# Fused attention, routed feed-forward and Mamba mixer: convolution taps, softplus halves and the last group's products reordered between VectorE, ScalarE and GpSimd

## The reference

```python
x = x + attention(layernorm(x))            # causal, one head
x = x + routed_ffn(layernorm(x))           # 8 experts, top tokens per expert
x = x + block(layernorm(x))                # x + mamba(layernorm(x)), then a dense FFN
x = x + routed_ffn(layernorm(x))           # the same weights again

def mamba(x):                              # d_inner 256, N 16, 4 taps, rank 64
    xm, z = split(x @ w_in)
    xm = silu(causal_conv4(xm) + b_conv)
    dt, Bc, Cc = split(xm @ w_xproj)       # 64, 16, 16 columns
    delta = softplus(dt @ w_dt + b_dt)
    h_t = exp(delta_t * A) * h_(t-1) + (delta_t * xm_t) * Bc_t
    y = sum_n(h * Cc) + xm * Dp
    return (y * silu(z)) @ w_out
```

## Time and profile before

| | us |
|---|---|
| median of 3 runs | 931.04 (930.60 to 931.06) |
| the profiled execution | 929.94 |
| its span, first to last instruction | 928.0 |
| routed layer's end and input stage | about 207 to 278 |
| softplus stage | about 278 to 325 |
| scan, 128 steps | 327.45 to 662 |

### The profile page before, as it was taken

The page is one execution under the profiler, slowest core; times in us unless marked ns, Lnnn a source line. Parts: engine busy times, 40 slices in busy tenths (PEclk is TensorE's granted clock), DMA queues, the critical chain, the costliest instruction groups (busy, mean ns, idle before and its releaser), DMA issues.

```text
span 928.0 us, 13935 instructions
## 1 busy us (share of the span) xinstructions
PE 639.2 (69%) x4284; PEld 509.3 (55%) x4285; DVE 695.0 (75%) x1721; ACT 562.6 (61%) x1180; POOL 453.2 (49%) x310
## 2 busy tenths in 40 slices
PE   3996026956989577878788787877799971169600
PEld 3785025842433267777677676776678760068500
DVE  7875873537844699999999999999987768844311
ACT  1566311324768989999999999999655535013200
POOL 4000007737300079898989888898610000057374
PEclk9998557987999889999999999999999995559955
DMA  8000302432000223233333333323500003014332
GB/s 225 10 1 1 91 0 63 110 63 54 24 2 6 38 69 103 98 103 95 103 102 103 95 100 103 102 99 101 166 1 1 1 1 91 0 43 102 80 97 81
DMA packets 61924, 63.33 MB, mean 68 GB/s; under 512 B 9095, under 2 KB 42698, under 8 KB 61866
## 3 DMA queue, kind: packets, MB, share of 16 engines
q1 hardware_dynamic: 57322, 53.30, 19.7%
q0 software_dynamic: 4544, 9.32, 4.7%
HBM read 50.92 MB, written 11.67 MB: 67 GB/s over the span
## 4 chain that ended last, share of the span: by engine, by line
DVE 30%; ACT 26%; PE 20%; POOL 12%; issue 8%; DMA 2%; DVEq 0%; POOLq 0%; SPq 0%; ACTq 0%
DVE work L1240 12%; ACT work L800 12%; POOL work L582 8%; ACT wfold L772 5%; POOL r_zs L587 5%; DVE work L994 4%; ACT dBuT L772 4%; PE bank L1698 3%; PE bank L1686 1%; PE decay_ps L1686 1%; PE decay_ps L1645 1%; PE bank L1458 1%; DMA work<-normed_rows,source 1%; DVE stats L899 1%; PE decay_ps L1408 1%
## 5 line engine op out<-in xcount | busy, mean ns | idle before, releaser
L1240 DVE TENSOR_TENSOR_SCAN work<-work,decay_ps 128x1024 f32<-128x1024 f32 x128 | 290.5, 2270 | 1.9 <-PE decay_ps L1602 1.9
L598 POOL TENSOR_TENSOR work<-work,C_bc 128x1024 f32<-128x1024 f32 x86 | 204.1, 2373 | 110.4 <-DVE work L1240 109.4
L582 POOL DMA_INDIRECT work<-normed_rows,source x78 | 75.2, 965 | 269.7 <-DVE source L1094 246.6
L800 ACT ACTIVATE work<-r_delta,Aneg 128x510 f32<-128x510 f32 x256 | 170.1, 713 | 9.0 <-DVE work L1240 7.5
L1615 PE MATMUL bank<-ident,work 128*128 128x128 f32 x1024 | 133.7, 274 | 0.1
L1615 PEld LDWEIGHTS bank<-ident,work 128*128 128x128 f32 x1024 | 116.7, 142 | 0.3 <-POOL work L598 0.3
L598 POOL TENSOR_TENSOR work<-work,win_s 128x1024 f32<-128x1024 f32 x42 | 99.7, 2375 | 11.2 <-DVE work L1240 11.2
L1602 PE MATMUL decay_ps<-ident,wfold 128*128 128x128 f32 x512 | 69.4, 279 | 37.5 <-DVE wfold L1232 24.8
L1602 PE MATMUL decay_ps<-ident,dBuT 128*128 128x128 f32 x512 | 69.5, 280 | 35.4 <-DVE dBuT L1232 35.4
L679 ACT ACTIVATE work<-bank 128x256 f32<-128x256 f32 x78 | 29.9, 383 | 92.0 <-PE bank L1478 89.0
L772 ACT ACTIVATE wfold<-duT,B_T 128x256 f32<-128x256 f32 x192 | 82.8, 495 | 1.4 <-PE decay_ps L1602 1.4
(11 more groups left out here) (267 smaller groups left out, 1277.7 us busy)
## 6 DMA issues: line engine op xcount, KB each, us to landing
C_bc<-routed_out SPq DMA_DIRECT2D x86, 256.0 KB, 3.1
win_s<-routed_out SPq DMA_DIRECT2D x42, 256.0 KB, 3.1
routed_out<-work SPq DMA_DIRECT2D x26, 192.0 KB
normed_rows<-r_zs SPq DMA_DIRECT2D x2, 2048.0 KB, 8.9
X<-in_L_attn_a_input_data SPq DMA_DIRECT2D x4, 512.0 KB, 5.8
r_du<-in_L_ffn_W SPq DMA_DIRECT2D x2, 1024.0 KB, 7.3
r_du<-in_L_ffn_W SPq DMA_DIRECT2D x4, 512.0 KB, 9.1
out<-X SPq DMA_DIRECT2D x8, 256.0 KB, 2.3
```

Of the source, the lines that this page charges most:

```text
L582: pool.indirect_dma_start(out=xin[:, i % 2, s, :], out_offset=None, in_=normed_rows, in_offset=bass.IndirectOffsetOnAxis(ap=source[:, k:k ...
L598: pool.tensor_tensor(h[:, m % 4], h[:, m % 4], col(C_bc[m % 3]).broadcast_to([P, NB, G]), ALU.mult).then_inc(c_hC, 1)
L800: last = A(o, d, ACT.Exp, scale=Aneg[:, b, n:n + 1])
L1240: V.tensor_tensor_scan(h[:, m % 4].rearrange("p b t -> p (b t)"), decay[:, m % 2].rearrange("p b t -> p (b t)"), decay_ps[:, m % 2].rearra ...
```

## The change

DVE's taps move behind the statistics of later groups: `later_taps(g - 4)` before `joined(g)` and `later_taps(g - 3)` behind `factors(g, 2)`, for g = 4 and 6; taps 4 to 6 come last. Block 1's Relu leaves ACT and becomes a DVE instruction from PSUM (`second_relu`); ACT takes Abs of block 1 first and signals it (`m_abs`). DVE's copies of the projections run one group ahead of the products (`projected(g + 1)` before `soft(g - 1)`). The last group's `delta` and `du` are made by POOL, and scan step 2 waits for that `delta`. ACT makes the first step's decay already in the iteration of group 6, before the last group's softplus.

```diff
--- before.py
+++ after.py
@@ -343,6 +343,8 @@
         s_c_rows = [sem(f"s_c_rows{s}") for s in range(2)]
         m_raw_ps = sem("m_raw_ps")
         m_raw = sem("m_raw")
+        m_abs = sem("m_abs")
+        m_relu = sem("m_relu")
         m_soft = sem("m_soft")
         m_delta = sem("m_delta")
         m_du = sem("m_du")
@@ -591,6 +593,16 @@
 
             routed(ffn[0])
 
+            last_soft, parts = tokens_of(NG - 1), (NG - 1) % 2
+            pool.wait_ge(m_delta, NG - 1)
+            pool.wait_ge(m_relu, NG)
+            pool.wait_ge(m_soft, NG)
+            pool.tensor_tensor(delta[:, :, last_soft], pos_part[parts], ln_part[parts], ALU.add).then_inc(m_delta, 1)
+            pool.wait_ge(m_delta, NG)
+            pool.wait_ge(m_du, NG - 1)
+            pool.tensor_tensor(du[:, :, last_soft], delta[:, :, last_soft], xm[:, :, last_soft],
+                               ALU.mult).then_inc(m_du, 1)
+
 
             for m in range(STEPS):
                 pool.wait_ge(c_h, m + 1)
@@ -735,15 +747,14 @@
                 if g > 1:
                     act.wait_ge(m_delta, g - 1)
                 act.wait_ge(m_raw_ps, g + 1)
-                for b in range(NB):
-                    ch.step(A(ln_part[s][:, b], bank[4 + 2 * s + b], ACT.Abs, bias=bdt_s[:, b:b + 1]))
-                for b in range(NB):
-                    last = A(pos_part[s][:, b], bank[4 + 2 * s + b], ACT.Relu, bias=bdt_s[:, b:b + 1])
-                last.then_inc(m_raw, 1)
+                A(ln_part[s][:, 1], bank[5 + 2 * s], ACT.Abs, bias=bdt_s[:, 1:2]).then_inc(m_abs, 1)
+                ch.step(A(ln_part[s][:, 0], bank[4 + 2 * s], ACT.Abs, bias=bdt_s[:, 0:1]))
+                A(pos_part[s][:, 0], bank[4 + 2 * s], ACT.Relu, bias=bdt_s[:, 0:1]).then_inc(m_raw, 1)
 
             def softened(g):
 
                 s = g % 2
+                act.wait_ge(m_abs, g + 1)
                 ch.wait()
                 ch.link(A(ln_part[s], ln_part[s], ACT.Exp, scale=-1.0))
                 A(ln_part[s], ln_part[s], ACT.Ln, bias=one_c[:, 0:1]).then_inc(m_soft, 1)
@@ -776,19 +787,8 @@
             second_block(NG - 1)
             act.preload_act_table_set("natural_log_exp_and_others")
             softened(0)
-            for g in range(1, NG):
-                folded(g)
-                softened(g)
-                if g >= NG - GT:
-                    if g < NG - 1:
-                        turned_du(0, g - (NG - GT))
-                if g == NG - 2:
-                    act.wait_ge(m_bt, 1)
-                    scaled(0)
-            act.wait_ge(m_bt, NG)
-            act.wait_ge(m_delta, NG - 1)
-            act.wait_ge(c_zero, 1)
-            for m in range(STEPS):
+            def decayed(m):
+
                 g, n = m // N, m % N
                 if m > 1:
                     act.wait_ge(c_h, m - 1)
@@ -799,6 +799,24 @@
                     o = decay[:, m % 2, b, :].rearrange("p (q t) -> p q t", q=GB)[:, :, 1:S]
                     last = A(o, d, ACT.Exp, scale=Aneg[:, b, n:n + 1])
                 last.then_inc(c_decay, 1)
+
+            for g in range(1, NG):
+                folded(g)
+                softened(g)
+                if g >= NG - GT:
+                    if g < NG - 1:
+                        turned_du(0, g - (NG - GT))
+                if g == NG - 2:
+                    act.wait_ge(m_bt, 1)
+                    scaled(0)
+                    act.wait_ge(m_delta, NG - 1)
+                    act.wait_ge(c_zero, 1)
+                    decayed(0)
+            act.wait_ge(m_bt, NG)
+            for m in range(STEPS):
+                g, n = m // N, m % N
+                if m > 0:
+                    decayed(m)
                 if m + 1 < STEPS:
                     scaled(m + 1)
                 if g + 1 < NG and n in DU_TURNS[0:GT - 1]:
@@ -1189,12 +1207,15 @@
                 factors(g, 1)
 
             for g in range(2, NG, 2):
+                if g > 2:
+                    later_taps(g - 4)
                 joined(g)
                 joined(g + 1)
                 factors(g, 2)
-                later_taps(g - 2)
-                later_taps(g - 1)
-            later_taps(NG - 2)
+                if g > 2:
+                    later_taps(g - 3)
+            for g in range(NG - 4, NG - 1):
+                later_taps(g)
 
             def projected(g):
 
@@ -1205,13 +1226,24 @@
                     dve.wait_ge(s_c_rows[g % 2], 16 * (g // 2))
                 V.tensor_copy(proj[0:PR, g % 2], bank[g % 2][0:PR, :]).then_inc(m_dt, 1)
 
-            def soft(g):
-
-                at = tokens_of(g)
+            def second_relu(g):
+
+                s = g % 2
+                dve.wait_ge(m_abs, g + 1)
+                V.tensor_scalar(pos_part[s][:, 1], bank[5 + 2 * s], bdt_s[:, 1:2], 0.0, ALU.add,
+                                ALU.max).then_inc(m_relu, 1)
+
+            def kept_b(g):
+
                 dve.wait_ge(m_bt_ps, g + 1)
                 V.tensor_copy(B_T[:, g * GT:(g + 1) * GT, :],
                               bank[2][:, 0:GT * PR].rearrange("p (q r) -> p q r", r=PR)[:, :, R:R + N]).then_inc(
                                   m_bt, 1)
+
+            def soft(g):
+
+                at = tokens_of(g)
+                dve.wait_ge(m_relu, g + 1)
                 dve.wait_ge(m_soft, g + 1)
                 V.tensor_tensor(delta[:, :, at], pos_part[g % 2], ln_part[g % 2], ALU.add).then_inc(m_delta, 1)
                 dve.wait_ge(m_delta, g + 1)
@@ -1219,8 +1251,12 @@
 
             projected(0)
             later_taps(NG - 1)
+            projected(1)
             for g in range(1, NG):
-                projected(g)
+                second_relu(g - 1)
+                kept_b(g - 1)
+                if g + 1 < NG:
+                    projected(g + 1)
                 soft(g - 1)
             V.memset(decay[:, :, :, 0:G:S], 0.0).then_inc(c_zero, 1)
 
@@ -1237,6 +1273,8 @@
                 dve.wait_ge(c_decay, m + 1)
                 if m > 3:
                     dve.wait_ge(c_y, m - 3)
+                elif m == 2:
+                    dve.wait_ge(m_delta, NG)
                 V.tensor_tensor_scan(h[:, m % 4].rearrange("p b t -> p (b t)"),
                                      decay[:, m % 2].rearrange("p b t -> p (b t)"),
                                      decay_ps[:, m % 2].rearrange("p b t -> p (b t)"), 0.0, ALU.mult,
@@ -1246,8 +1284,9 @@
                 dve.wait_ge(c_yd, NB * g + (b + 1))
                 V.tensor_tensor(xm[:, b, tokens_of(g)], bank[3], zs[:, b, tokens_of(g)], ALU.mult).then_inc(c_gated, 1)
 
+            second_relu(NG - 1)
+            kept_b(NG - 1)
             ch.step(V.tensor_scalar(gate[:, :], rs, 1.0, None, ALU.add))
-            soft(NG - 1)
             dve.wait_ge(m_bt, NG)
             for m in range(2):
                 scaled_last(m)
@@ -1562,6 +1601,8 @@
                     pe_.wait_ge(m_z, NG + 1)
                 pe_.wait_ge(m_dt, g + 1)
                 pe_.wait_ge(m_raw, g + 1)
+                if g > 1:
+                    pe_.wait_ge(m_relu, g - 1)
                 for b in range(NB):
                     last = mm(bank[4 + g % 2 * 2 + b], wdt_s[:, b * P:(b + 1) * P], proj[0:R, g % 2], start=True,
                               stop=True)
@@ -1597,6 +1638,7 @@
                     pe_.wait_ge(c_h, m - 1)
                 else:
                     pe_.wait_ge(m_raw, NG + 1 + m)
+                    pe_.wait_ge(m_relu, NG - 1 + m)
                 for k in range(GT):
                     for b in range(NB):
                         last = tr(decay_ps[:, m % 2, b, k * P:(k + 1) * P], dBuT[m % 2][:, k, b * P:(b + 1) * P],
```

## The result

The changed kernel took 918.89 us (median of 4 executions, 918.41 to 921.77), the kernel before 931.05; the ratio is 0.987 with a 95% interval of 0.9849 to 0.9891. Taken once more, beside its own runs of the kernel before, it took 919.17 against 930.06, 0.9882 [0.9867, 0.9898]. The forecast was 920.0 in a range of 918.0 to 924.0, so the time lies inside, and the parts can be read off one by one.

A forecast was written before the change was run, and what follows sets the result against it. No single engine: PE with waits in the input stage, a circle of ACT, DVE and PE in softplus, then scan(0)'s late start. 3.0 + 5.5 + 2.35 = 10.9 off the median 931.04 gives 920.1, stated 920.0; range 918.0 to 924.0.

The forecast's parts named there:

- Part 1: Input stage: with taps two groups back, groups 3 and 5 fall from 7.95 to 6.45 us; 3.0 us gained.
- the gap in group 1: Input stage: this PE gap stays, since its factors wait for group 3's gathered rows and no tap stands ahead.
- Part 2: Softplus stage, to_raw(0) to group 6's Ln end: 38.65 falls to 33.2 us, 5.5 gained, PE the bound.
- rival (c): Softplus stage: DVE becomes the bound, its Relu taking 0.96 us; +1.5, 921.5 us; chance 0.11.
- one fall: Softplus stage: one fall of PE's clock, a project taking 3.38 instead of 1.88, would take 1.5 us back.
- Rival (d): Softplus stage: PE runs groups at 1.2 GHz, 7.4 instead of 4.10 us; five of eight give 936.5; chance 0.04.
- Part 3: From S, the end of group 6's Ln, to scan(0): 11.25 us falls to 8.9, 2.35 gained.
- The margin at scan(4): Scan's head: what scan(4) needs is ready 1.7 us before its start at full clock, no margin at half.
- Rival (a): Scan's head: GpSimd's products cost 4.65 us, scan(4) and on wait for y sums; +2.8, 922.8 us; chance 0.09.
- The 1.3 that full clock at the end was to give: Before scan(0): PE's transposes were priced at half clock; at full clock 1.3 us more would be gained.
- the prediction's last line: Says the prediction is wrong if a covered wait ends last: ACT's for cleared columns or PE's for the Relu.

The follow-up runs named there:

- e1: The kernel before with only the new order of the convolution taps; 929.05 us, ratio 0.9968.
- e3: The kernel before with only block 1's Relu moved to DVE, projection copies still behind the products; 929.23 us, ratio 0.9972.
- e4: The kernel before with only the projection copies one group ahead, both Relus on ACT; 928.78 us, ratio 0.9964.
- e6: The changed kernel with the last group's two products back on DVE ahead of the first scan, first decay still early; 924.53 us, ratio 0.9927.
- e7: The changed kernel with the first decay back behind the last group's softplus; 917.39 us, ratio 0.985.
- e9: The changed kernel with GpSimd's du product made twice, 2.4 us more on GpSimd; 922.23 us, ratio 0.9913.
- e5: The kernel before with only the end edited: GpSimd makes the last group's two products, first decay early; 928.25 us, ratio 0.9969.
- e11: The changed kernel with five products nobody reads on PE ahead of its wait for the last copy of B; 919.48 us, ratio 0.9891.

## Why the prediction was right, step by step

**Part 1.** 3.0 forecast, 2.96 measured in a, 2.5 by e1's medians. No tap came late, and the gap in group 1 stayed for the reason given.

**Part 2.** 33.2 forecast for b, 32.88 or 32.89 measured in six of the nine executions that have this order; 5.77 gained instead of 5.5. PE is the bound at 4.11, with 4.10 forecast. The Relu was put at 0.68 and prints 0.74, 0.66 by spacing: the lower end of the bounds, and rival (c) with 0.96 is out. That it takes both edits was argued; e3 and e4 show it: with the Relu alone the circle stays closed, with the copies alone it opens and ACT, at 4.44 a group, takes PE's place. The remaining three executions (e6, e7, e9) took 34.53 to 34.58: `project(1)` ran at half clock behind the 1.17 us of idle time before `to_raw(0)`, which the change leaves. It is the "one fall" of the text, priced at 1.5 and measured at 1.65 to 1.70.

**The clock.** Here the argument was weaker than its result. The Trainium skill ("TensorE: Matmul & The Clock Gate", section on HAM oscillation), by which idle gaps lower the clock and steady work holds it, agrees with the changed kernel, whose stage ran at 1.00. But the three executions above have the same order and a fall at its start; that neither profiled execution of the change itself has one is luck, worth some 1.65 us. And a fall has no fixed price: in those three the clock was back after one `project`, while in e5 it stayed at half over 11 us of work without a gap, from 292.94 to 304.44, and b was 4.33 longer. Rival (d), held at 0.04, has a real mechanism. The change removes the gaps inside the stage that started it before; a full queue ended the fall soon in three executions and late in e5.

**Part 3.** S + 8.9 forecast for scan(0), S + 9.10 measured, 2.15 gained instead of 2.35; d says 1.74 and 2.13 in two executions. Terms: the decay at S + 2.6 forecast, S + 2.70 measured; group 7's softplus ends at S + 7.9, measured 317.00 + 1.15 = S + 7.88; GpSimd's delta done at S + 10.5, measured S + 10.42; its first product with C at S + 13.0, measured S + 12.80. The margin at scan(4) was given as 1.7 at full clock and none at half. The clock was half, and scan(4) waited 0.32 in one execution and not at all in the repeat; but what it waited for was PE's own transposes, with GpSimd about 0.9 ahead of them (e9). Rival (a) did not come about: both products cost 2.36 beside the scans, and its price of 4.65 was not seen. The 1.3 that full clock at the end was to give came to 1.13 at scan(0) and 0.54 at scan(8) in e11. And the prediction's last line counts ACT's wait for the cleared columns among the waits held to be covered, while its own sum has that wait on the path, at S + 2.6; the rows show it on the path, 1.04 long.

What the step missed is that the early decay, a part of the change whose wait was rightly priced at S + 2.6, is a loss against leaving it where it was. It was priced, but not against its alternative; with the rows that could have been done, since the path through the Abs, the Relu and the copy of B was written out in the text. Putting the copy of B ahead of the Relu was not tried.

**The sum.** 10.9 forecast, 10.87 from `in_proj(2)` to scan(0). The errors of the parts, -0.04, +0.27 and -0.20, nearly cancel, which is luck. To scan(8) the gain is 10.46, and 10.86 in the repeat. The text's own sum is 920.1 and is stated as 920.0. The remaining distance of 1.1 between 920.0 and 918.89 has, for the most part, another source: the profile before had 929.94 and its median 931.04. A sum made on the profiled execution gives 929.94 - 10.9 = 919.0; taking it off the median added 1.1. With the repeat, 930.06 - 10.9 = 919.2, and 919.17 was measured, so here the difference is only the spread of the kernel before.

## To carry to other kernels

Where a loop runs through three engines and none is full, an edit that opens the loop and one that shortens the next bound are worth more together than apart: 1.96 and 1.58 apart, 5.77 together, though some 1.5 of the surplus is one fall of the clock that either edit alone leaves in place. A step that is moved earlier on one engine is to be priced against the work behind it on that engine, and who waits for it: the early decay made its own step ready sooner and everything else 1.7 us later. And compare executions from a common point just ahead of the first edit, since parts that nobody touched moved by up to 3.1 us.

## What the hardware showed that was not expected

After a fall the granted clock can stay down while PE works without a gap: 0.50 over two windows of 4 us in which PE was busy all of the time (e5; columns as in the earlier trace rows):

```profile
294.00:298.00 4.00, 4.00 (x5) 1.19 (x5) 1.29 (x3) 2.93 (x4) 0.00 (x0) 0.50 0.04 8
298.00:302.00 4.00, 4.00 (x9) 1.56 (x8) 2.26 (x4) 1.64 (x3) 0.00 (x0) 0.50 0.04 8
```

The softplus stage in the changed order started at full clock in six executions and at half in three, with the same 1.17 us of idle time ahead of it. And the unedited work ahead of `in_proj(2)` took 233.0 to 236.1 us in the 14 profiled executions, a spread as large as the whole of part 1.
